# Scaling the row maxima and the softmax sums of a group-query attention on ScalarE instead of VectorE

## What is computed

```python
q = dequant_matmul(norm(x), qw_q, scales_q)        # 32 heads of 128
k, v = ...                                         # 8 groups of 128
q, k = rope(q), rope(k)
scores = einsum(q, k) / sqrt(128)                  # causal
attn = softmax(scores)
out = dequant_matmul(attn @ v, qw_o, scales_o)
```

## Time and profile before

| | |
|---|---|
| median of 3 runs | 1569.1 us (1567.02 to 1569.83) |
| the profiled execution | 1571.05 us |
| its span, from first to last instruction | 1569.2 us |
| TensorE busy | 1469.0 us, 94% |
| VectorE busy | 1237.7 us, 79% |
| ScalarE busy | 868.9 us, 55% |
| GpSimd busy | 237.6 us, 15% |
| mean granted clock of TensorE | 0.972 |

### The profile page before, as it was taken

One profiled execution on the slowest core, in us unless ns is written; L12 is line 12 of the kernel. 1 busy time (PEld: TensorE's weight loads), 2 busy tenths in 40 slices (PEclk: granted clock), 3 DMA queues, 4 the chain that ended last, 5 costly groups with the idle time before them and its releaser, 6 DMA issues.

```text
span 1569.2 us, 23528 instructions
## 1 busy us (share of the span) xinstructions
PE 1469.0 (94%) x7932; PEld 698.8 (45%) x7932; DVE 1237.7 (79%) x2583; ACT 868.9 (55%) x1468; POOL 237.6 (15%) x174
## 2 busy tenths in 40 slices
PE   5779999999999997899999999998999999999988
PEld 3412333333333354455555555554555555555534
DVE  4288888888886388787897887887887888878873
ACT  2205767676778324565665665664665665646630
POOL 2002000000000132221212212212212212211020
PEclk9957999999999998999999999999999999999989
DMA  3894000000000233566576575675684674653621
GB/s 97 150 143 134 1 1 0 0 0 0 0 0 11 64 94 98 105 140 144 121 137 139 120 150 127 129 147 120 128 160 111 141 145 110 134 96 67 115 54 54
DMA packets 352234, 144.64 MB, mean 92 GB/s; under 512 B 314680, under 2 KB 324408, under 8 KB 352128
## 3 DMA queue, kind: packets, MB, share of 16 engines
q1 hardware_dynamic: 352144, 143.48, 43.8%
HBM read 59.64 MB, written 6.19 MB: 42 GB/s over the span
## 4 chain that ended last, share of the span: by engine, by line
PE 73%; DVE 14%; ACT 6%; DMA 3%; issue 3%; SPq 0%; POOL 0%; DVEq 0%; ACTq 0%
PE ps L1433 9%; PE ps L1215 9%; PE ps L1435 9%; PE ps L1434 9%; PE ps L1268 7%; PE ps L1254 7%; PE ps L1395 4%; PE ps L1514 3%; PE ps L1516 3%; PE ps L1515 3%; ACT hl L680 2%; DVE hl L1038 2%; PE ps L1358 2%; DMA scratch<-pieces 2%; PE ps L1458 2%
## 5 line engine op out<-in xcount | busy, mean ns | idle before, releaser
L672 ACT ACTIVATE x<-ps,nmb,factor 128x128 f32<-128x128 f32 (+7 forms) x256 | 211.6, 832 | 290.9 <-DVE nmb L1023 290.9
L823 DVE TENSOR_REDUCE mx<-ps 128x1 f32<-128x512 f32 x512 | 326.4, 686 | 52.8 <-PE ps L1215 49.4
L581 ACT ACTIVATE proj<-ps 128x1024 f32<-128x1024 f32 x256 | 248.4, 1021 | 105.7 <-PE ps L1254 104.8
L1215 PE MATMUL ps<-ks,qs 96*128 (+1 forms) x512 | 200.1, 414 | 16.3 <-DVE mx L823 8.5
L1038 DVE SCALAR_TENSOR_TENSOR hl<-x,rden,hl 128x128 f16<-128x128 f32 (+7 forms) x256 | 208.3, 814 | 4.6 <-ACT hl L680 4.3
L680 ACT ACTIVATE hl<-x,rden 128x128 f16<-128x128 f32 (+7 forms) x256 | 184.1, 767 | 23.2 <-DVE rden L1034 22.5
L1021 DVE TENSOR_REDUCE nmr<-ps 128x1 f32<-128x128 f32 (+7 forms) x256 | 191.9, 750 | 0.0
L500 POOL TENSOR_TENSOR tmp<-tmp 128x640 f32<-128x640 f32 x64 | 98.4, 1538 | 532.1 <-DVE tmp L1017 532.1
L1433 PE MATMUL ps<-wh,xTh 128*128 128x256 f16 (+1 forms) x512 | 167.6, 327 | 0.0
L1434 PE MATMUL ps<-wl,xTh 128*128 128x256 f16 (+1 forms) x512 | 167.5, 327 | 0.0
L1435 PE MATMUL ps<-wh,xTl 128*128 128x256 f16 (+1 forms) x512 | 167.4, 327 | 0.0
(11 more groups left out here) (155 smaller groups left out, 2149.6 us busy)
## 6 DMA issues: line engine op xcount, KB each, us to landing
scale<-sp_n SPq DMA_DIRECT2D x32, 384.0 KB, 4.3
st<-in_L_attn_b_qw_q_dram SPq DMA_DIRECT2D x32, 256.0 KB, 2.8
st<-in_L_attn_b_qw_o_dram SPq DMA_DIRECT2D x32, 256.0 KB, 3.0
scale<-so_n SPq DMA_DIRECT2D x32, 256.0 KB, 3.6
qs<-scratch SPq DMA_DIRECT2D x24, 256.0 KB, 8.4
hlT<-hl SPq DMA_TRANSPOSE x256, 3.5
scratch<-pieces SPq DMA_DIRECT2D x5, 768.0 KB, 13.4
xnat<-attn_a_hidden_state_dram SPq DMA_DIRECT2D x8, 256.0 KB, 4.8
```

Of the source, the lines that this page charges most:

```text
L581: nc.scalar.activation(pbuf[:, e % 4, :].rearrange("p (b n) -> p b n", b=2), ps[:, b:b + 2, :], ACT.Exp, scale=float(HD) ** -0.5).then_inc ...
L672: nc.scalar.activation(pr[:, h, 0:n], flat(2 * (h % 2), n), ACT.Exp, bias=nmb[:, h:h + 1], scale=factor[:, par, 0:1], accum_out=den[:, h:h ...
L823: nc.vector.tensor_reduce(mx[:, f, k // 2, k % 2:k % 2 + 1], ps[:, bank(k), :], AX.X, ALU.max).then_inc(s_mx, 1)
L1215: mm(ps[:, bank, :], qs[0:STACK, ds(g * R + h, 1), f * HALF + qt * P:f * HALF + (qt + 1) * P], ks[0:STACK, ds(g, 1), kh * HALF:(kh + 1) * ...
```

## The change

The product with the group's factor (256 instructions, one for each head and step) and the scaling of the sums (128 instructions, one for each pair of heads and step) go from VectorE to ScalarE. The scaled sums get a small tensor of their own, `sums_scaled`, taken from an unused gap, so that nothing else moves in memory. The semaphores keep their meaning: the maximum signals `s_mxb`, the product `s_nb`, the exponential `s_eb`, the scaling `s_dn`, the inverse `s_rd`.

```diff
@@ ScalarE, exponentials(h) and after it
+                    act.wait_ge(s_mxb, u * R + h + 1)
+                    nc.scalar.activation(nmb[:, h:h + 1], nmr[:, h:h + 1], ACT.Copy,
+                                         scale=factor[:, par, 0:1]).then_inc(s_nb, 1)
                     act.wait_ge(s_nb, u * R + h + 1)
                     nc.scalar.activation(pr[:, h, 0:n], flat(2 * (h % 2), n), ACT.Exp, bias=nmb[:, h:h + 1],
                                          scale=factor[:, par, 0:1], accum_out=den[:, h:h + 1]).then_inc(s_eb, 1)
+
+                def sums(a):
+                    act.wait_ge(s_eb, u * R + 2 * a + 2)
+                    nc.scalar.activation(sums_scaled[:, 2 * a:2 * a + 2], den[:, 2 * a:2 * a + 2], ACT.Copy,
+                                         scale=1.0 / PSCALE).then_inc(s_dn, 1)
...
                 exponentials(0)
                 exponentials(1)
+                sums(0)
...
                 exponentials(2)
                 exponentials(3)
+                sums(1)
@@ VectorE, maximum(u, h, n) and invert(u, a)
-                dve.wait_ge(s_mxb, u * R + h + 1)
-                nc.vector.tensor_scalar(nmb[:, h:h + 1], nmr[:, h:h + 1], factor[:, par, 0:1], None,
-                                        ALU.mult).then_inc(s_nb, 1)
...
-                dve.wait_ge(s_eb, u * R + 2 * a + 2)
-                nc.vector.tensor_scalar(rden[:, 2 * a:2 * a + 2], den[:, 2 * a:2 * a + 2], 1.0 / PSCALE, None,
-                                        ALU.mult).then_inc(s_dn, 1)
                 dve.wait_ge(s_dn, u * 2 + a + 1)
-                nc.vector.reciprocal(rden[:, 2 * a:2 * a + 2], rden[:, 2 * a:2 * a + 2]).then_inc(s_rd, 1)
+                nc.vector.reciprocal(rden[:, 2 * a:2 * a + 2], sums_scaled[:, 2 * a:2 * a + 2]).then_inc(s_rd, 1)
```

More of the change, by code:

```diff
@@ L165, in build @@
             rden = scoped(mem, "rden", [P, R])
-            scoped(mem, "gap", [P, P])
+            sums_scaled = scoped(mem, "sums_scaled", [P, R])
+            scoped(mem, "gap", [P, P - R])
             wh, wl = (scoped(mem, f"w{c}", [P, 2, KC, BW], F16) for c in "hl")
@@ L1017, in rope_sin, with maximum @@
                 nc.vector.tensor_tensor(o[:, :, HALF_D:], rotary_in()[:, :, 0:HALF_D], sn, ALU.mult).then_inc(s_rope, 1)
-            def maximum(u, h, n, par):
+            def maximum(u, h, n):
                 dve.wait_ge(s_sc, u * R + h + 1)
                 nc.vector.tensor_reduce(nmr[:, h:h + 1], flat(2 * (h % 2), n), AX.X, ALU.max, negate=True).then_inc(s_mxb, 1)
-                dve.wait_ge(s_mxb, u * R + h + 1)
-                nc.vector.tensor_scalar(nmb[:, h:h + 1], nmr[:, h:h + 1], factor[:, par, 0:1], None,
-                                        ALU.mult).then_inc(s_nb, 1)
             def group_factor(g, par):
@@ L1077, in step @@
                     dve.wait_ge(s_fcr, g + 1)
-                maximum(u, 0, n, par)
+                maximum(u, 0, n)
                 if exists(*one):
@@ L1085, in step @@
                     rope_sin(t2)
-                maximum(u, 1, n, par)
+                maximum(u, 1, n)
                 invert(u, 0)
@@ L1089, in step @@
                     values_low(u + 1, par if t < T - 1 else 1 - par, t2)
-                maximum(u, 2, n, par)
+                maximum(u, 2, n)
                 low(u, 0, n)
-                maximum(u, 3, n, par)
+                maximum(u, 3, n)
                 if not end:
```

## The result

| | before | after |
|---|---|---|
| median of the runs | 1569.1 us (5 runs, 1566.47 to 1569.83) | 1585.41 us (5 runs, 1584.54 to 1585.91) |
| ratio to before | | 1.0102, 95% interval 1.0084 to 1.0121 |
| span of the profiled execution | 1569.2 | 1583.6 |
| time from one group to the next (values product of step 0, group after 1066.32) | 110.95 | 112.71 |

The kernel became 1.0% slower, by 16.3 us. The forecast was 1582, in a range of 1571 to 1593.

The account below looks back on a forecast made before the run. TensorE, busy 94%, was taken as bound, with a VectorE-ScalarE loop behind its waits growing 0.53 us a step. Eight groups late by 1.7, less 0.75, gave +12.8 on 1569.1: 1582 us, range 1571 to 1593.

Parts of the forecast that it names:

- ScalarE's prices: Costs on ScalarE in attention B: 0.286 us for a product with per-partition operand, 0.203 for scaling the sums.
- own wait: An engine's wait for its own previous instruction; 0.035 us on VectorE, the same taken for ScalarE.
- Rival 1: ScalarE's small instructions all short, product 0.203 without operand surcharge: +1 to +2 us, 1570.5; chance 0.13.
- rival 3: ScalarE's wait for its own instruction 0.1 instead of 0.035, five a step: +26 us, 1595; chance 0.13.
- The walk through the group: Attention B, steps 0 to 7: delays summed place by place, from -0.25 in step 0 to 1.7 us at group's end.
- The early gains: Steps 0 to 3: work earlier than before, -0.25 at step 0's values product, -0.31 and -0.17 at later scores.
- the loop: VectorE and ScalarE handing work to each other from one rotary embedding to the next; longer by 0.53 us a step.
- Eight groups of 1.7 less a tail of 0.75: Whole kernel: eight late groups make 13.6 us, VectorE's tail after the last step saves 0.75; sum +12.8.
- Rival 2: VectorE's relief decides if ScalarE hides its small instructions under exponentials: about -0.6 a group, -5 us, 1564; chance 0.06.

Follow-up runs that it names:

- the filled pair: Kernels before and after, each computing head 2's scores five times instead of once in each group's step 0: 1568.19 us and 1580.57 us.
- the filling: Head 2's scores computed five times instead of once in each group's step 0; added to the kernel with the scalings alone on ScalarE: 1569.84 us.

## Why the prediction was right, and where it wasn't

The sign, the size and the mechanism came as forecast; 1582 was said and 1585.4 measured. By its own steps:

1. **ScalarE's prices.** Product 0.286 forecast, 0.290 measured; scaling 0.203 and 0.203; own wait 0.035 and 0.033. The reading from far rows (392 ns for 128 columns, 1140 for 1024, taken down to one column) held; that the operand is what makes the difference is shown by the run with a fixed scale. Rival 1 fell with this number, rival 3 with the own wait. VectorE's scaling, put at 0.17, has a mean of 0.201, but takes 0.15 to 0.17 from step 2 on. The Trainium skill, page "ScalarE: Activation LUTs", section "What ACT_TABLE_LOAD costs", says that each pointer operand adds about 93 ns; the trace agrees with 92 (290 less 198).

2. **The walk through the group.** As delays against before, from VectorE's low part 2 ahead of step 0 (1057.82 before, 1066.49 after: 8.67, the zero of this table) to the same in the next group:

| place | start before | start after | delay over 8.67 | forecast |
|---|---|---|---|---|
| low part 3 (VectorE) | 1059.47 | 1067.89 | -0.25 | -0.25 |
| step 0, values product | 1066.32 | 1074.90 | -0.09 | -0.25 |
| step 2, head 0's scores | 1082.75 | 1091.29 | -0.13 | -0.31 |
| step 3, head 0's scores | 1094.45 | 1103.23 | +0.11 | -0.17 |
| step 4, head 0's scores | 1106.77 | 1116.03 | +0.59 | +0.51 |
| step 5, head 0's scores | 1119.90 | 1129.41 | +0.84 | +0.75 |
| step 5, head 3's scores | 1129.48 | 1139.08 | +0.93 | +0.92 |
| step 6, head 3's scores | 1144.36 | 1154.28 | +1.25 | +1.26 |
| step 7, head 3's scores | 1160.53 | 1170.64 | +1.44 | +1.47 |
| low part 2 of the next group | 1168.90 | 1179.21 | +1.64 | +1.7 |

The two rows of VectorE's next group are these, of before and of after:

```profile
1168.90 1.28 DVE L1038 SCALAR_TENSOR_TENSOR hl<-x,rden,hl 128x1024 f16<-128x1024 f32 x1 [0.27 <-ACT hl L680]
```

```profile
1179.21 1.28 DVE L1043 SCALAR_TENSOR_TENSOR hl<-x,rden,hl 128x1024 f16<-128x1024 f32 x1
```

From step 4 on each place is within 0.1. The embeddings of steps 3 to 7 are late by 0.24, 0.77, 1.31, 1.67 and 1.59, where 0.25, 0.78, 1.31, 1.69 and 1.64 were forecast. For the last two the walk lets idle time absorb 0.13 and, by its own figures, 0.58 that its rows don't show, and the low part of k in step 5 was late by 1.16 where it had 1.42: there the agreement is better than the working. TensorE's wait before step 4 was forecast at 0.9, for the exponential; it is 0.84, for the exponential. The period is 112.7, 112.8 forecast.

3. **The early gains were too large** by 0.16 to 0.28, in steps 0 to 3. Low part 3 does come 0.25 earlier, by VectorE's freed product, but the values product only 0.09: its transposed operand takes 5.74 us from the end of that low part (1069.16 to 1074.90) where it took 5.57 (1060.75 to 1066.32), and TensorE's wait for it grew from 0.27 to 0.62. In step 3 (1.19) the wait is the exponential's already, one step sooner than the walk had it. Neither reaches the end: in step 4 the loop is what counts, and it overtakes both. Beside it, TensorE's start behind such a read-out was put at 0.05 us, and at head 0's scores it is 0.15 (1115.88 to 1116.03), a tenth more in step 4. That head 0's product alone was worth about 0.1 us a group says the same as the first.

4. **Eight groups of 1.7 less a tail of 0.75** made 12.8; the filled pair gives 12.4. The terms aren't quite those: in the filled pair seven periods grow by 13.0 together, and in the last group, where VectorE has no weights to dequantise, the delay doesn't grow (9.88 at its first values product after step 0, 9.71 at its last, and 9.7 in the spans). The last group was overcharged by 1.7, the tail's gain of 0.75 isn't there, and seven groups at 1.86 in place of 1.7 bring 1.1 more. These errors nearly cancel, which is luck.

5. **What was missing** is the clock. The prediction costs no fall of TensorE's clock, and the profiled execution has one, 1.7 us. Besides, the sum is right for the profiled pair (12.7 beside the fall), and the medians are 2 us further apart than the profiles. The measured time stayed in the range because the range was made for other unknowns.

6. **Rival 2**, that VectorE's relief decides, was partly tested and fell: products 2 and 3 alone lose, product 0 alone gains about 0.1 a group, and so do the scalings alone with the filling (110.76 to 110.87 against 110.87 to 110.94). Its condition, product and wait together under 0.15, isn't met: they take 0.32 and nothing overlaps them.

## What to carry to other kernels

Shares of busy time say little about where a small instruction may go. Two engines that hand work to each other form a loop, and an instruction moved between them stays in it, at the other's price and with another wait; here 0.214 on one became 0.32 on the other, twice in a row where nothing ran beside it. Find out which of the loop's instructions can vanish instead, and whether it is needed at all.

When a change makes TensorE's short idle times come differently, look at the granted clock right behind them, by windows of a few us, and at the number of matmuls in each: a slowed matmul counts as busy. If the clock falls, a few redundant matmuls in the idle time are a cheap test, and sometimes the cure.

## What wasn't expected of the hardware

TensorE's clock falls to its lower level (a granted 0.57 over 4 us) behind the idle times of step 0, at a cost of some 1.7 us. In the profiled executions this happened in none of seven groups before, one after the change, two with the four products alone, six with the scalings alone, three with products 2 and 3, two with product 0, six with product 0 and the first scaling, four without the operand and four without scaling; and in none of 35 in the five kernels with the filling. These are one execution of each kernel, and the recorded clocks above say that their number changes from one execution to the next. The filling needn't fill all: more than half of the idle time remains (0.16, 0.42 and 0.59 us in the changed kernel, filled, against 1.05, 0.42 and 0.62). The sum of idle time doesn't tell which: in the group shown before has more (1.98 us) than the scalings alone (1.80), and no fall. Nor do the single waits. The unscaled kernel with head 0's product has a fall in every other group, and the waits before it are the same, for the exponential 0.76 and 0.77, for the transposed probabilities as in these rows, with a fall at the first (15.45 us to the values product of step 1) and none at the second (13.77):

```profile
954.63 0.48 PE L1548 MATMUL ps<-hlT,vh 128*128 128x512 f16 x1 [0.87 <-DMA hlT<-hl]
...
1066.43 0.38 PE L1548 MATMUL ps<-hlT,vh 128*128 128x512 f16 x1 [0.85 <-DMA hlT<-hl]
```

What decides between them stays open. The Trainium skill, page "TensorE: Matmul & The Clock Gate", section "A second HAM failure mode: psum-queue depth-cycling", tells, of a kernel that cycles through PSUM banks, of short idle times between groups of matmuls that make the clock go up and down; the runs agree in so far as the falls come behind such idle times, at 1.7 us each, and stayed away where the longest was filled.

VectorE's scaling of two columns takes 0.57 us in step 0 before (1064.21 to 1064.78) and ends with GpSimd's addition there (1063.23 to 1064.76); in step 1, where it also starts under that addition and ends with it, it takes 0.34, and from step 2 on 0.15 to 0.17. ScalarE's takes 0.20 in every step. These two steps are the one place where the move was a gain, too small to show in the time.
